# Products of probabilities and values in four column tiles of 32 in place of two of 64

## The chip, the cores and the metric

The kernel runs on one core of one Trainium2 chip. The metric is the device time of one execution in microseconds. The kernel before was timed three times: 3240.45, 3241.63 and 3242.56 us, median 3241.63 us.

## What is computed

The input x has the shape 32 x 56 x 56 x 96 (images, rows, columns, channels), all in float32. Two blocks follow each other; this change touches the first.

```python
x = x + _L0_conv_ref(_gn(x), qkv_w, qkv_b, proj_w, proj_b, rel_table)   # shifted window attention
x = x + _L1_conv_ref(_gn(x))                                            # ratio of box sums
```

The core of the first block, with windows of 7 x 7 (L = 49 tokens), 12 heads and d = 8 channels for each head:

```python
qkv = xw @ qkv_w.T + qkv_b                 # xw: 32 * 64 windows, 49 tokens, 96 channels
q = q * d ** (-0.5)
attn = einsum('bhqd,bhkd->bhqk', q, k) + bias + mask
attn = softmax(attn, axis=-1)
out = einsum('bhqk,bhkd->bhqd', attn, v)   # the product that the change touches
out = out @ proj_w.T + proj_b
```

The second block takes sums over 5 columns and sums over 20 channels of the normalised image and of its square, and adds their ratio.

## The kernel before, in words

The work is cut three ways. An image has 8 units, each a row of 8 windows. A unit has 4 steps, each a pair of windows (w = 0 and w = 1). So there are 32 x 8 x 4 = 1024 steps. A window's 49 tokens lie on partitions 0 to 48, the other window's on 64 to 112.

The program is a software pipeline written out by hand. One loop over slots (L587 on TensorE, and the same loop on each of the other engines) issues in each slot the stages of different steps, in a fixed order; a semaphore per stage holds an engine until its input is there. On TensorE a slot s is, in this order:

- `times_v(s-3)` (L475 to L489): the product of probabilities and values of a step. It writes `pO`, for each of 6 pairs of heads and each of the two windows one matmul: the stationary operand is `P32` (128 rows, the 49 queries of one head for the weights' columns), the moving operand is `V` (18 columns: 8 channels and a one for each of two heads). So 12 matmuls a step, each with its own weights. All operands are float32; the trace shows two weight loads and two matmuls for each matmul of the program, 24 of each a step. The output of window 0 goes to the partitions 0 to 48, that of window 1 to 64 to 112, which are two column tiles of 64 of the array.
- `scores(s+1)` (L446 to L462): 8 bfloat16 matmuls into `pS`, in column tiles of 64 too; first the four of window 0, then the four of window 1. It waits for `biased`, by which VectorE tells that it has read the scores of the step before.
- every fourth slot `values` (L423 to L444): 48 bfloat16 matmuls with 49 columns of weights, which alternate between the two column tiles of 64.
- `turn_scores(s-1)` (L464 to L473): 6 transposes with 128 columns of weights, over the whole width of the array.
- then work that comes once in four slots, all over the whole width: loading and turning x (L394), the box sums (L555, L561, L572, L581), the turned output (L500), the projections (L400 to L402, L510), and small matmuls of the normalisation (L516, L521, L528).

VectorE adds the bias and finds the maximum of the step's scores (L820, L827), GpSimd subtracts it (L1050), ScalarE takes the exponentials into `P32` (L662) and copies from PSUM. Of `pO` nobody reads before the four steps of a unit are done: then VectorE takes the reciprocal of the sums and divides (L850, L857).

Of the kernel before, what the change touches and what calls it, by code (L numbers as in the profile page):

```python
# [15 lines left out]
L = WIN * WIN  # L16
# [10 lines left out]
VC = 2 * (D + 1)  # L27
# [102 lines left out]
def build(nc, x, wT, bias_row, pT, pb_row, flipped, consts, out):  # L130
    ctx = ExitStack()
    with ctx:
        def sb(name, shape, dt=F32):
            return ctx.enter_context(nc.sbuf_tensor(name, shape, dt))

        def psum(name, shape):
            return ctx.enter_context(nc.psum_tensor(name, shape, F32))
# [34 lines left out]
        V = [sb(f"V{i}", [128, UNITS, HP, 2, D + 1]) for i in range(2)]  # L172
        T = [sb(f"T{i}", [128, HEADS, 64]) for i in range(4)]
        MX = [sb(f"MX{i}", [128, HEADS]) for i in range(4)]
        P32 = [sb(f"P32{i}", [128, HEADS, L]) for i in range(3)]
# [27 lines left out]
        pO = psum("pO", [128, 512])  # L203
# [178 lines left out]
        def _(pe):  # L382
# [92 lines left out]
            def times_v(j):  # L475

                U, p = divmod(j, PAIRS)
                pe.wait_ge(p_made, j + 1)
                if p == 0:
                    pe.wait_ge(v_kept, 2 * U + 2)  # L480
                    if U:

                        pe.wait_ge(o_made, U)
                for h in range(HP):
                    col = VC * (HP * p + h)
                    for w in range(2):
                        mm = pe.matmul(pO[64 * w:64 * w + L, col:col + VC], P32[j % 3][:, 2 * h + w, :],  # L487
                                       V[U % 2][:, 2 * p + w, h, :, :], start=True, stop=True)
                mm.then_inc(pv_made, 1)  # L489

            def turn_o(U):
# [95 lines left out]
            for s in range(FIRST_SLOT, END_SLOT + 1):  # L587
                for j in steps(s - 3):
                    times_v(j)
# [515 lines left out]
```

## Time and profile before

| | |
|---|---|
| time of an execution, median of 3 | 3241.63 us |
| span of the profiled execution (first to last instruction) | 3240.4 us |
| TensorE busy | 3157.0 us, 97% |
| VectorE busy | 2883.8 us, 89% |
| ScalarE, GpSimd busy | 70% each |
| granted TensorE clock | 1.00 from 70 to 3160 us |

The profiled execution has no time of its own beside its span; the span stands 1.2 us under the median and inside the three times. PE is TensorE's matmuls, PEld its weight loads. The recorded length of a matmul includes its way through the array (a float32 matmul of 18 moving columns is shown with 200 ns), so lengths of matmuls overlap and their sum tells little. What TensorE spends on a block is read as the difference between the start of the block and the start of the next one in the view in order of time.

### The profile page before, as it was taken

How to read it: one execution, taken by the hardware profiler on the slowest of the kernel's cores; microseconds unless marked ns; L12 is line 12 of the kernel's file. 1: busy time of each engine (PE TensorE's matmuls, PEld its weight loads, DVE VectorE, ACT ScalarE, POOL GpSimd, SP SyncE). 2: the span in 40 equal slices, each digit the busy share in tenths (PEclk: the TensorE clock that was granted, in tenths of full speed). 3: DMA queues.
4: the chain of work that ended last, by engine and by line, in shares of the span. 5: the costliest groups of instructions: out<-in, count | busy, mean ns of one | idle time of the engine just before them, and what ended most of it. 6: DMA issues, size and time to landing. Idle time of an engine off the chain costs nothing.

```text
span 3240.4 us, 146752 instructions
## 1 busy us (share of the span) xinstructions
PE 3157.0 (97%) x60544; PEld 2668.2 (82%) x60544; DVE 2883.8 (89%) x4882; ACT 2282.5 (70%) x4705; POOL 2267.1 (70%) x2522
## 2 busy tenths in 40 slices
PE   4999999999999999999999999999999999999997
PEld 3888888888888888888888888888888888888885
DVE  5999999999999999999999999999999999999983
ACT  2577777777777777777777777777777777777764
POOL 4677777777777777777777777777777777767763
PEclk8999999999999999999999999999999999999995
DMA  3333333333333333333333333333333333333320
GB/s 85 93 84 94 86 89 90 91 87 90 91 87 89 95 85 87 93 89 87 95 86 87 94 88 88 88 92 87 90 93 85 88 95 86 88 97 75 77 65 24
DMA packets 385696, 280.19 MB, mean 86 GB/s; under 512 B 261931, under 2 KB 384908, under 8 KB 385036
## 3 DMA queue, kind: packets, MB, share of 16 engines
q1 hardware_dynamic: 384652, 270.69, 33.9%
q8 instruction: 485, 7.95, 1.1%
q14 instruction: 175, 1.43, 0.1%
q10 hardware_dynamic: 384, 0.11, 0.0%
HBM read 39.35 MB, written 38.54 MB: 24 GB/s over the span
## 4 chain that ended last, share of the span: by engine, by line
PE 92%; ACT 3%; SPq 2%; issue 1%; DVE 1%; DMA 0%; ACTq 0%; POOL 0%; DVEq 0%; POOLq 0%
PE pP L472 22%; PE pO L487 19%; PE pS L460 9%; PE pM L555 6%; PE pM L572 5%; PE pM L510 5%; PE pM L442 5%; PE pM L561 5%; PE pM L394 3%; PE pM L500 3%; PE pM L400 3%; PE pM L401 3%; PE pM L402 3%; PE pM L581 2%; SPq L335 1%
## 5 line engine op out<-in xcount | busy, mean ns | idle before, releaser
L1050 POOL TENSOR_TENSOR T<-T,MX 128x588 f32<-128x588 f32 x1024 | 1212.3, 1185 | 889.8 <-DVE MX L827 886.8
L662 ACT ACTIVATE P<-pP 128x588 f32<-128x588 f32 x1024 | 673.7, 658 | 418.4 <-PE pP L472 411.9
L820 DVE TENSOR_TENSOR T<-pS,table 128x588 f32<-128x588 f32 x1024 | 783.5, 765 | 82.4 <-PE pS L460 53.8
L472 PE MATMUL pP<-K,T 113*128 113x113 f32 x6144 | 818.9, 269 | 0.8 <-ACT P L662 0.8
L827 DVE TENSOR_REDUCE MX<-T 128x12 f32<-128x588 f32 x1024 | 778.3, 760 | 25.9
L487 PEld LDWEIGHTS pO<-V,P 128*49 128x49 f32 x24576 | 646.2, 125 | 162.4 <-ACT P L662 69.2
L487 PE MATMUL pO<-V,P 128*49 128x18 f32 x24576 | 747.1, 200 | 0.4 <-DVE O L857 0.4
L472 PEld LDWEIGHTS pP<-K,T 113*128 113x128 f32 x6144 | 602.6, 141 | 93.3 <-issue 1.0
L460 PE MATMUL pS<-KE,QS 128*64 128x196 bf16 (+1 forms) x8192 | 466.4, 231 | 17.3 <-DMA KE<-KS 16.3
L767 ACT ACTIVATE rd<-pM,tiny 112x384 f32<-112x384 f32 x224 | 130.3, 582 | 362.1 <-PE pM L561 362.0
L460 PEld LDWEIGHTS pS<-KE,QS 128*64 128x64 bf16 x8192 | 309.8, 110 | 18.6 <-DMA KE<-KS 17.0
L652 ACT ACTIVATE V<-pM 49x384 f32<-49x384 f32 x512 | 262.9, 514 | 45.4 <-PE pM L442 39.1
L572 PEld LDWEIGHTS pM<-K,ybox 96*112 96x112 f32 x1792 | 217.9, 183 | 69.5 <-issue 5.9
L1027 POOL TENSOR_TENSOR ybox<-y,Y 96x448 f32<-96x448 f32 x224 | 254.6, 1137 | 17.6
L1015 POOL TENSOR_TENSOR y<-Y 96x472 f32<-96x472 f32 x224 | 217.5, 971 | 41.1 <-ACT Y L739 38.8
L1011 POOL TENSOR_TENSOR XL<-X,XH 96x392 bf16<-96x392 f32 x256 | 238.3, 931 | 0.0
L555 PE MATMUL pM<-K,SQ 96*112 96x96 f32 x1792 | 217.6, 266 | 3.0 <-DVE numt L913 1.9
L572 PE MATMUL pM<-K,ybox 96*112 96x96 f32 x1792 | 216.0, 265 | 0.0
L907 DVE SCALAR_TENSOR_TENSOR numt<-pM,rd 112x384 f32<-112x384 f32 x224 | 125.0, 558 | 100.5 <-PE pM L572 54.1
L510 PE MATMUL pM<-OT,PT 97*96 97x392 f32 x512 | 211.1, 493 | 1.9 <-DVE numt L913 1.9
L1020 POOL TENSOR_TENSOR y<-y 96x448 f32<-96x448 f32 x224 | 208.5, 931 | 0.7
L442 PE MATMUL pM<-WHV,XH 97*49 97x48 bf16 x4096 | 196.1, 184 | 12.6 <-ACT OT L671 12.6
(94 smaller groups left out, 5976.6 us busy)
## 6 DMA issues: line engine op xcount, KB each, us to landing
KE<-KS SPq DMA_DIRECT2D x512, 147.0 KB
KS<-knh SPq DMA_DIRECT2D x768, 49.0 KB
QS<-qnh SPq DMA_DIRECT2D x768, 49.0 KB
out<-tok_out SPq DMA_DIRECT2D x384, 84.0 KB
tok_in<-x SPq DMA_DIRECT2D x224, 84.0 KB
KS<-knl SPq DMA_DIRECT2D x384, 49.0 KB
QS<-qnl SPq DMA_DIRECT2D x384, 49.0 KB
tok_in<-x SPq DMA_DIRECT2D x224, 63.0 KB
```

Of the source, the lines that this page charges most:

```text
L442: mm = pe.matmul(bankA[64 * h:64 * h + L, col:col + C // 2], lhs, wv[:, :, h, :], start=(part == 0), stop=(part == 2))
L460: mm = pe.matmul(pS[64 * w:64 * w + 64, bank, col:col + (h1 - h0) * L], Q[:, gq, at:at + 64], E[:, h0:h1, at:at + L], start=True, stop=True)
L472: mm = pe.transpose(pP[:, c, QN * at:QN * at + QN], T[j % 4][0:QN, 2 * h:2 * h + 2, :], pick)
L487: mm = pe.matmul(pO[64 * w:64 * w + L, col:col + VC], P32[j % 3][:, 2 * h + w, :], V[U % 2][:, 2 * p + w, h, :, :], start=True, stop=True)
L510: pe.matmul(bankB[0:C, 0:TOK], PT[:, :], OT[:, :], start=True, stop=True).then_inc(proj_made, 1)
L555: mm = pe.matmul(bankB[0:ROWS2, C * t:C * t + C], SQ[:, ROWS2 * t:ROWS2 * t + ROWS2], band, start=True, stop=True)
L572: mm = pe.matmul(bankC[0:ROWS2, C * t:C * t + C], ybox2[:, ROWS2 * t:ROWS2 * t + ROWS2], band, start=True, stop=True)
L652: act.activation(V[U % 2][ps, :, :, h, 0:D], bankA[ps, 0:PAIRS * C].rearrange("p (w a d) -> p w a d", w=UNITS, d=D), ACT.Copy).then_inc(v_ ...
L662: act.activation(P32[j % 3][:, :, :].rearrange("p (c a w) q -> p c a (w q)", c=2, w=2), src, ACT.Exp).then_inc(p_made, 1)
L820: dve.tensor_tensor(T[j % 4][:, :, 0:L].rearrange("p (b h) k -> p b h k", b=2), pS[:, :, 0:HALF].rearrange("p b (h k) -> p b h k", k=L), t ...
L827: dve.tensor_reduce(MX[j % 4][:, :], T[j % 4][:, :, 0:L], AX.X, ALU.max).then_inc(maxed, 1)
L1050: pool.tensor_tensor(t, t, MX[j % 4][:, :].unsqueeze(2).broadcast_to([128, HEADS, L]), ALU.subtract).then_inc(shifted, 1)
```

## The change

Each of the 12 matmuls of a step with 49 columns of weights becomes two: one with the queries 0 to 31 (32 columns of weights), one with the queries 32 to 48 (17 columns). The outputs go to the same places in `pO`; window 0 now uses the column tiles of 32 at partitions 0 and 32, window 1 those at 64 and 96. The moving operand is the same, and is streamed for each of them.

```diff
                     for w in range(2):
-                        mm = pe.matmul(pO[64 * w:64 * w + L, col:col + VC], P32[j % 3][:, 2 * h + w, :],
-                                       V[U % 2][:, 2 * p + w, h, :, :], start=True, stop=True)
+                        for q0, q1 in ((0, 32), (32, L)):
+                            mm = pe.matmul(pO[64 * w + q0:64 * w + q1, col:col + VC], P32[j % 3][:, 2 * h + w, q0:q1],
+                                           V[U % 2][:, 2 * p + w, h, :, :], start=True, stop=True)
                 mm.then_inc(pv_made, 1)
```

No semaphore, buffer or stage moves, and the other engines' programs are the same. Only TensorE's list of instructions differs. In the order of the program, TensorE before, around one product (the first figure of a form is the number of weight columns, the second that of moving columns):

```order
L572 MATMUL pM<-K,ybox 112x96 x4
L500 MATMUL pM<-K,O 96x113 x4
L487 MATMUL pO<-V,P 49x18 x12
L460 MATMUL pS<-KE,QS 64x196
L460 MATMUL pS<-KE,QS 64x98 x2
```

This is the order that a step has: full-width work, one group of 12 with equal forms, and at once the scores.

In the changed kernel, where such a product begins (lines after L487 are one further on: L501 is L500, L573 is L572):

```order
L573 MATMUL pM<-K,ybox 112x96 x4
L501 MATMUL pM<-K,O 96x113 x4
L488 MATMUL pO<-V,P 32x18
L488 MATMUL pO<-V,P 17x18
L488 MATMUL pO<-V,P 32x18
L488 MATMUL pO<-V,P 17x18
```

The work ahead is unchanged; the product now opens with a 32-column matmul of window 0 and its 17-column rest, then the same for window 1. And where it ends and the scores begin:

```order
L488 MATMUL pO<-V,P 32x18
L488 MATMUL pO<-V,P 17x18
L460 MATMUL pS<-KE,QS 64x196
L460 MATMUL pS<-KE,QS 64x98 x2
L460 MATMUL pS<-KE,QS 64x196 x2
```

So the 12 matmuls of a step are 24, of 32 and 17 columns in turn, and what stands before and behind them is the same; the scores behind them stay in column tiles of 64.

## Rows read from the trace of the kernel before

**Rows 1.** The page, parts 1 and 2: busy time, and the granted TensorE clock by slices.

```profile
PE 3157.0 (97%) x60544; PEld 2668.2 (82%) x60544; DVE 2883.8 (89%) x4882; ACT 2282.5 (70%) x4705; POOL 2267.1 (70%) x2522
...
PEclk8999999999999999999999999999999999999995
```

**Rows 2.** The page, part 4: the chain of waits that ended last, by engine and line.

```profile
PE 92%; ACT 3%; SPq 2%; issue 1%; DVE 1%; DMA 0%; ACTq 0%; POOL 0%; DVEq 0%; POOLq 0%
PE pP L472 22%; PE pO L487 19%; PE pS L460 9%; PE pM L555 6%; PE pM L572 5%; PE pM L510 5%; PE pM L442 5%; PE pM L561 5%; PE pM L394 3%; PE pM L500 3%; PE pM L400 3%; PE pM L401 3%; PE pM L402 3%; PE pM L581 2%; SPq L335 1%
```

**Rows 3.** Stretches (start-up, middle, tail): busy us (x instructions) by engine, PE clock, DMA.

```profile
core 0: us, PE busy (x) PEld busy (x) DVE busy (x) ACT busy (x) POOL busy (x), PEclk, DMA share, GB/s
0.00:70.00 70.00, 25.72 (x175) 17.15 (x176) 33.47 (x49) 18.05 (x41) 27.74 (x44) 0.88 0.33 81
70.00:3160.00 3090.00, 3073.65 (x60107) 2607.30 (x60107) 2825.64 (x4788) 2229.34 (x4597) 2211.65 (x2449) 1.00 0.36 88
3160.00:3240.40 80.40, 57.62 (x272) 43.74 (x268) 24.71 (x47) 35.08 (x69) 27.67 (x30) 0.55 0.09 24
```

**Rows 4.** The waits: engine and line waiting, releaser, us in total, times, longest.

```profile
POOL T L1050 <- DVE MX L827: 886.8, 737, 35.5
...
DVE T L820 <- PE pS L460: 53.8, 221, 10.2
...
PE pS L460 <- DMA KE<-KS: 16.3, 5, 13.8
```

**Rows 5.** The page, part 5: groups of instructions (columns as the page's heading says).

```profile
L487 PEld LDWEIGHTS pO<-V,P 128*49 128x49 f32 x24576 | 646.2, 125 | 162.4 <-ACT P L662 69.2
L487 PE MATMUL pO<-V,P 128*49 128x18 f32 x24576 | 747.1, 200 | 0.4 <-DVE O L857 0.4
```

**Rows 6.** TensorE in order of time: start us, us, engine, line, instructions merged.

```profile
1602.36 0.55 PE L500 MATMUL pM<-K,O 113*96 113x113 f32 x4
1602.84 0.73 PE L487 MATMUL pO<-V,P 128*49 128x18 f32 x24
1603.41 0.46 PE L460 MATMUL pS<-KE,QS 128*64 128x196 bf16 x8
1603.67 0.21 PE L442 MATMUL pM<-WHV,XH 97*49 97x48 bf16 x2
...
1604.28 0.18 PE L442 MATMUL pM<-WHV,XL 97*49 97x48 bf16 x1
1604.28 0.18 PE L442 MATMUL pM<-WLV,XH 97*49 97x48 bf16 x1
1604.31 0.18 PE L442 MATMUL pM<-WHV,XL 97*49 97x48 bf16 x1
1604.42 0.80 PE L472 MATMUL pP<-K,T 113*128 113x113 f32 x6
1605.06 0.82 PE L510 MATMUL pM<-OT,PT 97*96 97x392 f32 x2
...
1606.14 0.73 PE L487 MATMUL pO<-V,P 128*49 128x18 f32 x24
1606.71 0.46 PE L460 MATMUL pS<-KE,QS 128*64 128x196 bf16 x8
1607.10 0.80 PE L472 MATMUL pP<-K,T 113*128 113x113 f32 x6
1607.73 0.33 PE L400 MATMUL pM<-XH,WH 97*96 97x392 bf16 x1
...
1610.42 0.55 PE L394 MATMUL pM<-K,tok_in 112*96 112x112 f32 x4
1610.80 0.94 PE L555 MATMUL pM<-K,SQ 96*112 96x96 f32 x8
1611.67 0.50 PE L487 MATMUL pO<-V,P 128*49 128x18 f32 x14
```

**Rows 7.** Groups by form: weight loads of 112, 49 (bf16) and 96 columns.

```profile
L555 PEld LDWEIGHTS pM<-K,SQ 96*112 96x112 f32 x1792 | 199.9, 183 | 5.2 <-issue 4.4 <-ACT g L695 0.8
...
L442 PEld LDWEIGHTS pM<-WLV,XH 97*49 97x49 bf16 x4096 | 175.2, 103 | 0.0
...
L510 PEld LDWEIGHTS pM<-OT,PT 97*96 97x96 f32 x512 | 67.0, 164 | 2.5 <-issue 2.1
```

**Rows 8.** Groups by form: the scores' matmuls, wide and narrow.

```profile
L460 PE MATMUL pS<-KE,QS 128*64 128x196 bf16 x4096 | 466.4, 256 | 17.3 <-DMA KE<-KS 16.3 <-DVE T L820 0.9
L460 PE MATMUL pS<-KE,QS 128*64 128x98 bf16 x4096 | 285.0, 206 | 0.0
```

## The prediction

> **What bounds the kernel now.** I first read busy shares, then the chain of waits, then the waits themselves, then TensorE in order of time. TensorE is busy 97% of the span at the full granted clock of 2.4 GHz, VectorE 89% [rows 1]. The chain that ended last runs 92% of the span through TensorE, and the line that changes, L487, holds 19% of it, the second largest share [rows 2]. Between 70 and 3160 us TensorE is idle only 3090.0 - 3073.7 = 16 us; VectorE is idle 3090.0 - 2825.6 = 264 us there [rows 3]. The long waits are those of others for TensorE or for each other; TensorE's own longest is 16.3 us for the first transfers, and VectorE waits 53.8 us in all for the scores [rows 4]. So TensorE is the bound throughout: what a step saves or costs on its engine comes through nearly one to one, until VectorE's 264 us are used up.
>
> **What a product costs now.** The busy sums don't tell it: 24576 matmuls of 200 ns would be more than the whole span, they lie over each other [rows 5]. The starts do. A product begins at 1602.84 and the scores behind it at 1603.41: 0.57 us for 24 matmuls; 1606.14 to 1606.71 again [rows 6]. Two things about this 0.57 us decide the case.
>
> First, the two column tiles run side by side. The scores are written as four matmuls of window 0 and then four of window 1, 4 x 196 + 4 x 98 = 1176 moving columns [rows 8], which at 2.4 GHz in a line are 0.49 us; they take 0.26 us (1603.41 to 1603.67) [rows 6]. So TensorE takes the second tile's work ahead while the first is busy. In the product each tile then has 12 load-and-matmul pairs in 0.57 us, 47.5 ns each.
>
> Second, it is the weight load that sets these 47.5 ns. The 18 moving columns are fewer than the 49 columns of weights. A float32 load grows with its columns: 125 ns recorded for 49 [rows 5], 164 for 96, 183 for 112 [rows 7]. In spacing rather than in recorded length: the eight loads of 112 columns at L555 take 1610.80 to 1611.67, 0.87 us, of which 0.095 us is the change of tiling worked out below, so 97 ns each against 47.5 ns for 49 columns: (97 - 47.5) / 63 = 0.79 to 0.81 ns for a column [rows 6].
>
> **The change, part by part.** (a) Narrower loads. A tile with 32 columns saves 17 x 0.81 = 13.8 ns in each of its 12 slots of time: 33.7 ns in place of 47.5. The tiles with 17 columns need 47.5 - 32 x 0.81 = 21.6 ns and are done before, if all four tiles run side by side. Saving 12 x 13.8 = 166 ns a step.
>
> (b) Twice as many instructions, 48 load-and-matmul pairs a step in place of 24. Within 12 x 33.7 = 404 ns that is one pair each 8.4 ns. No row shows such a pace. The nearest is L442, 48 pairs whose starts lie between 1603.67 and 1604.31, 0.64 us for 47 spacings, 13.6 ns each, and there two tiles' matmuls start at the same hundredth (both at 1604.28) [rows 6]; a tile's own spacing is 27 ns there, close to what 49 bfloat16 columns need, so 13.6 ns is a pace that was reached and not a limit that was met. Bounds for the product: 404 ns if the pace is no limit (a little less if narrow tiles had a lower floor than I assume, 12 x 27 = 324 ns), and 48 x 13.6 = 653 ns if 13.6 ns were the least. I take the 404, because the equal starts speak against a shared minimum and because the engine was seen to run different tiles independently.
>
> (c) One more change of tiling. The product is bracketed today by full-width work ahead and by the scores behind, which use the same column tiles of 64. Before a change of tiling a block gets longer: four transposes of 112 columns (L394) take 1610.42 to 1610.80 when full-width work follows, four of 113 (L500) take 1602.36 to 1602.84 when the product follows: 0.38 and 0.48 us; starts are shown to 10 ns, so the loss is 0.09 to 0.11, and I take 0.095. And the six transposes at L472 right behind such a change take 1604.42 to 1605.06, 0.64 us, where 6 x 0.096 = 0.58 would do: up to 0.055 us more for a first load that nothing hides [rows 6]. From the product to the scores there is no such loss now. With tiles of 32 in front of tiles of 64 there would be one in each step. Bounds: 0 (as between equal tilings) and 0.095 + 0.055 = 0.15 us. I take 0.095 + 0.020, since the scores' load is half as wide as L472's, and about 10 ns for four tiles in place of two that have to be started one after another: 125 ns.
>
> Here a rule of the Trainium skill bears. What the rows show is the loss between tiles of 64 and the full width. TensorEngine Tiling, Key Properties, states it in general: a change of the tiling mode, not just of the tile, drains the engine. The trace agrees where it can; whether 32 after 64 counts as such a change no row shows. By the rule the term is the 125 ns above, without it about 10 ns.
>
> Nothing else moves: no wait is added, `pO` is read by VectorE only once in four steps, and the same semaphore is raised by the last matmul. The granted clock should stay at 2.4 GHz, for TensorE works without a pause before and after.
>
> **Sum.** A step: -166 + 125 = -41 ns. 1024 steps: -42 us. VectorE's 264 us of slack cover it, so all of it should come through. From the profiled execution's 3240.4 us: 3198 us; the median of the runs stands 1.2 us above that, so 3200 us.
>
> **The rivals.** *No loss between tiles of 64 and 32.* Step: -166 + 10 = -156 ns, 160 us in all. For it: both are column tilings over all 128 rows, and a tile of 64 covers just two of 32. Against it: the loss at the full width. VectorE's work would then be 2826 of some 2930 us and would begin to hold single steps, so I take nine tenths: 3241.6 - 144 = about 3097 us.
>
> *A common pace of loads and matmuls.* The place is the product alone; the price is 48 x pace against 570 ns before, plus the 125 ns. It decides from 48 x pace = 570 - 125, or 9.3 ns a pair: above it the kernel gets slower. At 13.6 ns: 653 + 125 - 570 = +208 ns a step, +213 us, 3455 us; at 11 ns +85 us, 3327 us. The same comes out if only two tiles can take weights at a time: 12 x (33.7 + 21.6) = 664 ns. For it: nowhere in the trace do more than two column tiles work at a time. Against it: the equal starts.
>
> Beside this rival: TensorE: Matmul & The Clock Gate, in its table of the isolated gap, puts a floor of about 25 ns on the start-to-start time of small matmuls. If it held over all tiles the product would take 48 x 25 = 1200 ns, a step 1200 + 125 - 570 = 755 ns more and the kernel 4015 us, an estimate from that page; the trace disagrees, since L442 starts one each 13.6 ns [rows 6], and only a floor within one tile is left of it, which 33.7 ns respects.
>
> *Gain and loss cancel.* With a pace near 9 ns, or the extra change at its full 0.15 us and a tile of 32 at 37 ns, the sum is zero: 3241 us. That the change doesn't do what it says is excluded by the order: the forms 32x18 and 17x18 alternate.
>
> **How the numbers follow.** The forecast of some -10 to -75 us (around 3200 us, its own range 3165 to 3230) gets 0.46. No loss between the tilings 0.15. Common pace above 9.4 ns 0.27, spread from 3250 to 3460 us. Cancelling 0.12. About 0.2%, 6.5 us, is what a measurement of this kernel can tell from no change. Faster: 0.46 + 0.15, less 0.01 for its edge, 0.60; same 0.12; slower 0.28. The range leaves out the upper half of the pace case and a little below the second: 3090 to 3345 us.
>
> **What would show it.** Right: product to scores about 0.52 us (0.40 for the loads, the rest the loss) in place of 0.57, four tiles' matmuls in bundles 34 ns apart, the loads of 32 columns recorded with about 111 ns and those of 17 with 99, scores and transposes behind them unchanged. The loss between tilings shown wrong: 0.41 us from product to scores. The pace shown: 0.65 us or more, with single matmuls evenly spaced. What would make the prediction wrong elsewhere: TensorE idle before L460 or L472 in the middle stretch, which would be VectorE's or ScalarE's doing.

## The result and the profile after

The changed kernel takes 3227.30 us (median of 4 runs, 3223.82 to 3230.10), the kernel before in the same job 3241.36 us (3240.45 to 3242.56). The ratio is 0.9955, with a 95% interval of 0.9943 to 0.9968: faster by 14 us or 0.45%, a third of the 42 us that were forecast. One thing is seen before any trace is opened: the runs of before lie within 2.1 us of each other, those after within 6.3 us.

The page after (parts 1, 3, 4 and 5; of queue q8, which brings the instructions, the columns are packets, MB, share of 16 engines):

```profile
PE 3123.7 (97%) x85120; PEld 2599.5 (81%) x85120; DVE 2870.6 (89%) x4882; ACT 2282.8 (71%) x4705; POOL 2267.8 (70%) x2522
...
q8 instruction: 677, 11.09, 1.5%
...
PE 93%; ACT 3%; issue 2%; DVE 1%; ACTq 0%; SPq 0%; POOL 0%; DMA 0%; POOLq 0%; DVEq 0%
PE pP L472 23%; PE pO L488 16%; PE pS L460 12%; PE pM L556 6%; PE pM L573 5%; PE pM L511 5%; PE pM L442 5%; PE pM L562 5%; PE pM L394 3%; PE pM L501 3%; PE pM L400 3%; PE pM L401 3%; PE pM L402 3%; PE pM L582 2%; PE pM L529 1%
...
L488 PE MATMUL pO<-V,P 128*32 128x18 f32 (+1 forms) x49152 | 610.5, 184 | 13.5 <-issue 12.5
```

and q8 on the page before:

```profile
q8 instruction: 485, 7.95, 1.1%
```

TensorE is still the bound, 93% of the chain [rows 2]. The changed line went from 19% to 16% of it, the scores behind it from 9% to 12%. A cause of idle time has come up at L488 that had none there before: 12.5 us of "issue", time in which TensorE waited for nothing that the profile shows. And 192 more packets of instructions were fetched. TensorE has 49152 more loads and matmuls than before, and q8 has 3.14 MB more: 64 bytes an instruction, 256 instructions a packet.

The middle stretch, for [rows 3]:

```profile
70.00:3145.00 3075.00, 3040.91 (x84627) 2538.61 (x84626) 2812.30 (x4786) 2229.45 (x4596) 2212.37 (x2449) 1.00 0.37 90
```

TensorE is idle 34 us there against 16, while VectorE's share is what it was.

TensorE in order of time, two undisturbed products, for [rows 6]:

```profile
1604.98 0.33 PE L402 MATMUL pM<-XH,WL 97*96 97x392 bf16 x1
1605.24 0.59 PE L488 MATMUL pO<-V,P 128*32 128x18 f32 x48
1605.76 0.46 PE L460 MATMUL pS<-KE,QS 128*64 128x196 bf16 x8
1606.15 0.80 PE L472 MATMUL pP<-K,T 113*128 113x113 f32 x6
1606.79 0.55 PE L394 MATMUL pM<-K,tok_in 112*96 112x112 f32 x4
1607.17 0.94 PE L556 MATMUL pM<-K,SQ 96*112 96x96 f32 x8
1608.04 0.59 PE L488 MATMUL pO<-V,P 128*32 128x18 f32 x48
1608.56 0.46 PE L460 MATMUL pS<-KE,QS 128*64 128x196 bf16 x8
1608.95 0.80 PE L472 MATMUL pP<-K,T 113*128 113x113 f32 x6
```

From the product to the scores it is 0.52 us both times (1605.24 to 1605.76, 1608.04 to 1608.56) where it was 0.57. From the scores to the transposes it is 0.39 us as before, or finely 8 ns more. The weight loads by form (mean ns behind the busy us), for [rows 5]:

```profile
L488 PEld LDWEIGHTS pO<-V,P 128*32 128x32 f32 x24576 | 505.0, 110 | 170.9 <-ACT P L663 69.2 <-issue 59.5
L488 PEld LDWEIGHTS pO<-V,P 128*17 128x17 f32 x24576 | 488.6, 95 | 8.1 <-issue 7.8
```

110 ns for 32 columns and 95 for 17, against 125 for 49.

Over the whole trace, by the differences of the blocks' starts: the median of 1020 products went from 571 to 520 ns; the scores before transposes from 385 to 393 (767 times), before values from 265 to 286 (255 times), the values from 748 to 734. In sum -52.0 + 6.1 + 5.4 - 3.6 = -44 us. The spans differ by 14.6 us. So 29.5 us were gained and lost again, and not in the usual step. The next view shows where; it is a product that took 1.60 us in place of 0.52:

```profile
1354.23 0.55 PE L501 MATMUL pM<-K,O 113*96 113x113 f32 x4
1354.71 0.44 PE L488 MATMUL pO<-V,P 128*32 128x18 f32 x32
1356.07 0.31 PE L488 MATMUL pO<-V,P 128*32 128x18 f32 x16 [0.92 <-issue]
1356.31 0.46 PE L460 MATMUL pS<-KE,QS 128*64 128x196 bf16 x8
```

In the middle of it, between two matmuls that wait for no semaphore, TensorE stood for 0.92 us. Such waits come up in the view of waits (us in total, times, longest). The trace before has not one row of this kind ("issue") for the matmuls:

```profile
PE pO L488 <- issue: 12.5, 24, 1.0
...
PE pS L460 <- issue: 4.1, 9, 1.0
...
PE pM L442 <- issue: 1.5, 3, 0.7
...
PE pP L472 <- issue: 0.4, 1, 0.4
```

A recorded matmul runs on for 0.18 us after its start, so that each idle time is shown shorter than the stall was, and short ones not at all. Measured from start to start, there are 58 gaps between 0.17 and 1.16 us beyond the usual spacing (the median of the same pair of forms), 28.8 us in all: the missing sum. All 58 stand at the same place: when the loads, matmuls and semaphore instructions of TensorE's program are counted, the instruction behind the gap is the 197th to 204th of a group of 256, nearly all the 197th to 199th. In the trace before, the gaps of this size are spread over all places, and are the waits at the start of an image. 256 instructions are one packet of q8, and the program of TensorE has as many such groups as q8 has packets: 677 after, 485 before.

### The profile page after: what moved, and what is told of

Read it like the earlier page. It is cut to its first block, busy times and chain, and to the rows that moved or that the text cites. A ratio compares the mean times of both kernels' runs of the same rounds, so it can differ in the third digit from the quotient of the medians.

```text
span 3225.8 us, 195904 instructions
## 1 busy us (share of the span) xinstructions
PE 3123.7 (97%) x85120; PEld 2599.5 (81%) x85120; DVE 2870.6 (89%) x4882; ACT 2282.8 (71%) x4705; POOL 2267.8 (70%) x2522
## 4 chain that ended last, share of the span: by engine, by line
PE 93%; ACT 3%; issue 2%; DVE 1%; ACTq 0%; SPq 0%; POOL 0%; DMA 0%; POOLq 0%; DVEq 0%
PE pP L472 23%; PE pO L488 16%; PE pS L460 12%; PE pM L556 6%; PE pM L573 5%; PE pM L511 5%; PE pM L442 5%; PE pM L562 5%; PE pM L394 3%; PE pM L501 3%; PE pM L400 3%; PE pM L401 3%; PE pM L402 3%; PE pM L582 2%; PE pM L529 1%
## 5 line engine op out<-in xcount | busy, mean ns | idle before, releaser
L472 PE MATMUL pP<-K,T 113*128 113x113 f32 x6144 | 820.0, 270 | 2.1 <-ACT P L663 1.0
L472 PEld LDWEIGHTS pP<-K,T 113*128 113x128 f32 x6144 | 603.1, 141 | 95.4 <-issue 2.7
L488 PEld LDWEIGHTS pO<-V,P 128*17 128x17 f32 (+1 forms) x49152 | 505.6, 103 | 179.0 <-ACT P L663 69.2
L488 PE MATMUL pO<-V,P 128*32 128x18 f32 (+1 forms) x49152 | 610.5, 184 | 13.5 <-issue 12.5
L460 PE MATMUL pS<-KE,QS 128*64 128x196 bf16 (+1 forms) x8192 | 478.0, 234 | 19.9 <-DMA KE<-KS 14.3
L460 PEld LDWEIGHTS pS<-KE,QS 128*64 128x64 bf16 x8192 | 292.9, 109 | 53.2 <-DMA KE<-KS 14.5
L573 PEld LDWEIGHTS pM<-K,ybox 96*112 96x112 f32 x1792 | 217.9, 183 | 69.5 <-issue 6.2
L573 PE MATMUL pM<-K,ybox 96*112 96x96 f32 x1792 | 216.0, 265 | 0.0
```

The lines of the kernel that those rows point to most:

```text
L460: mm = pe.matmul(pS[64 * w:64 * w + 64, bank, col:col + (h1 - h0) * L], Q[:, gq, at:at + 64], E[:, h0:h1, at:at + L], start=True, stop=True)
L472: mm = pe.transpose(pP[:, c, QN * at:QN * at + QN], T[j % 4][0:QN, 2 * h:2 * h + 2, :], pick)
L488: mm = pe.matmul(pO[64 * w + q0:64 * w + q1, col:col + VC], P32[j % 3][:, 2 * h + w, q0:q1], V[U % 2][:, 2 * p + w, h, :, :], start=True, ...
L573: mm = pe.matmul(bankC[0:ROWS2, C * t:C * t + C], ybox2[:, ROWS2 * t:ROWS2 * t + ROWS2], band, start=True, stop=True)
```

## The experiments

Theory A, formed from this: TensorE runs out of instructions. A group of 256 must last until the next one is fetched and usable. In the 56 stalled groups that could be measured, the packet was fetched 1.7 us (median) after the group before was begun, took 1.0 us, and TensorE went on 1.4 us after its end, together some 4.2 us. Before, the quickest of all groups lasted 4.4 us; after, the quickest lasts 3.3 us. From the 20th group on, TensorE begins no group in any trace of this case sooner than 1.1 us after the end of the packet that was fetched during the group ahead; in the trace before, the least is 2.0 us, so that it never came near this bound. A quick group need not stall: most of those under 4.2 us did not, and their fetch began earlier (0.4 us after the group's beginning, median, against 1.6 to 1.7 in the stalled ones). The theory's rival B: the time is lost by the four tiles themselves, by the changes of tiling, or by other engines that fall behind. All ratios are to the kernel before, timed in the same job, and each edit is one of the changed kernel unless it is said otherwise. The stalls are told from one profiled execution of each kernel.

**24 products of 32 columns** (the count of instructions as before, tiles of 32).

```diff
-                        for q0, q1 in ((0, 32), (32, L)):
+                        for q0, q1 in ((0, 32),):
```

> Leaves out the queries 32 to 48 of each product, so a step has 24 load-and-matmul pairs of 32 columns, as many instructions as before, in tiles of 32. Theory A (instruction supply): the changed kernel lost about 27 us in some 56 stretches in which TensorE had used up its instructions; with the count of before these go. The product's block stays at 0.50 to 0.52 us, no idle time of TensorE put down to issue at L488, time 3185 to 3202 us. Theory B (the lost time comes from the four tiles, the changes of tiling or other engines falling behind, not from the number of instructions): the long blocks stay in part, time 3210 us or more.

Measured: 3174.17 us, ratio 0.9793 (0.9779 to 0.9806). In order of time:

```profile
1602.91 0.56 PE L488 MATMUL pO<-V,P 128*32 128x18 f32 x24
1603.41 0.46 PE L460 MATMUL pS<-KE,QS 128*64 128x196 bf16 x8
1603.80 0.80 PE L472 MATMUL pP<-K,T 113*128 113x113 f32 x6
```

The block takes 0.50 us (median of all 490 ns), and there is no idle time put down to issue for any matmul. The time is under the range that A gave, since the block was 30 ns shorter than the one with four tiles; B's 3210 us is excluded. This kernel has half the instructions in the product, but also two tiles in place of four; which of the two takes the stalls away the next experiments tell.

**24 products of 33 columns** (the same, in tiles of 64).

```diff
-                        for q0, q1 in ((0, 32), (32, L)):
+                        for q0, q1 in ((0, 33),):
```

> Leaves out the queries 33 to 48 of each product: 24 pairs of 33 columns, which need column tiles of 64 as before, and so no further change of tiling before the scores. If the change of tiling costs about 0.1 us a step and the load of 33 columns is as good as that of 32: the block takes 0.41 to 0.42 us against 0.50 to 0.52 with 32 columns alone, time 3080 to 3105 us. If a change between tiles of 64 and 32 costs nothing and the loads themselves are slower than forecast: 0.50 us here too, and 3185 to 3200 us.

Measured: 3109.78 us, ratio 0.9602 (0.9587 to 0.9617).

```profile
1602.08 0.57 PE L488 MATMUL pO<-V,P 128*33 128x18 f32 x24
1602.49 0.45 PE L460 MATMUL pS<-KE,QS 128*64 128x196 bf16 x8
1602.87 0.80 PE L472 MATMUL pP<-K,T 113*128 113x113 f32 x6
```

0.41 us from product to scores, 0.08 less than with 32 columns, although each load is one column wider. So there is a price for going from tiles of 32 to tiles of 64: 490 - 411 + 10 for the wider column in 12 loads + 8 in the scores, 0.10 us in all. And 16 columns fewer in 12 loads gave 571 - 411 = 160 ns, 0.83 ns a column. The step's gain, 164 us over 1024 steps, did not all come through: the total fell by 131 us. The scores before the values became longer, from 265 to 333 ns; I put this down to the values, which now wait for ScalarE's copies. The trace bears it out: the first weight load of the values starts 113 to 115 ns behind the end of the copy at L672 in nearly all units, where it is 151 ns (median) in the trace of before. No run tests it.

**32 columns and 1** (instructions and tiles as after, hardly any work in two of the tiles).

```diff
-                        for q0, q1 in ((0, 32), (32, L)):
+                        for q0, q1 in ((0, 32), (32, 33)):
```

> Leaves out the queries 33 to 48: each product is issued as 32 columns and 1 column, with as many instructions and the same tiles as in the changed kernel, but next to no work in the second and fourth tile. Theory A: the same stalls, 20 to 30 us of idle time put down to issue, time 3217 to 3230 us. Theory B, in the form that the loads of 17 columns crowd out those of 32: the stalls go, 3185 to 3200 us.

Measured: 3234.47 us (3228.89 to 3243.66), ratio 0.9979 (0.9969 to 0.9990).

```profile
PE pO L488 <- issue: 13.5, 24, 1.2
...
PE pS L460 <- issue: 3.9, 10, 0.6
...
PE pM L442 <- issue: 3.1, 6, 0.8
```

The stalls are all there, 71 gaps with 34 us at the same place of the groups of 256, and the block is 520 ns, as with 17 columns. Between this kernel's span and that of the one with 32 columns alone stand 62.5 us: 31 us for a block that is 30 ns longer, and 32 us more of stalls (34 against 2 at most), for 24576 more loads and as many more matmuls with a single column. The width of the added matmuls doesn't matter. That it is their number, and not the four tiles, is shown by the place in the groups of 256 and by the runs that follow. It came out 4 us above the range that A gave, the number of stalls being greater than I had assumed.

**The second step of each unit undivided.** The slot of this product also has the 48 matmuls of the values.

```diff
-                        for q0, q1 in ((0, 32), (32, L)):
+                        for q0, q1 in (((0, L),) if p == 1 else ((0, 32), (32, L))):
```

> Complete. The product of the second step of each unit, which stands in the slot with the 48 matmuls of the values and so in the densest stretch of instructions, stays undivided (49 columns, two tiles of 64); the other three are divided. Theory A: three quarters of the steady gain of 43 us a kernel (32 us) and hardly a stall: 3207 to 3213 us, faster than both. Theory B: three quarters of the gain measured, about 3231 us.

Measured: 3215.77 us, ratio 0.9924 (0.9911 to 0.9936).

```profile
PE pO L488 <- issue: 0.6, 2, 0.4
...
PE pP L472 <- issue: 0.6, 1, 0.6
```

Faster than both kernels, with a quarter fewer divided products. 15 gaps with 5.7 us are left; for 9 of them, 3.3 us, TensorE goes on within 1.7 us of the end of a packet, as in the stalls above. It is 3 us above A's range and 15 under B's value.

**The first step undivided instead**, the same number of instructions in the program.

```diff
-                        for q0, q1 in ((0, 32), (32, L)):
+                        for q0, q1 in (((0, L),) if p == 0 else ((0, 32), (32, L))):
```

> Complete. As p1_undivided, but it is the first step's product in each unit that stays undivided; as many instructions and as much steady gain, only the slot differs: this one has no values. If the stalls come from the number of instructions as such: 3216 us, like p1_undivided. If they come from dense stretches (the slot with the values and the one before it): more stalls than p1_undivided, 8 to 18 us of them, 3218 to 3226 us.

Measured: 3235.96 us (3231.76 to 3240.55), ratio 0.9982 (0.9973 to 0.9991).

```profile
PE pO L488 <- issue: 5.8, 16, 0.8
...
PE pM L442 <- issue: 3.4, 6, 1.0
...
PE pS L460 <- issue: 2.7, 6, 0.8
```

44 gaps with 21 us. Both kernels have the same instructions in number and kind, and differ by 19 us (by the ratios; they were timed in different jobs) by where the dense ones stand. It is not the sum of instructions that matters, but how quickly 256 in a row are used up. The median lies above my range, and even the profiled execution, 33 us of steady gain less 21 of stalls, comes to a span of 3228 by this sum against the measured 3231.9; so I can't account for the last few microseconds.

**Two divided products together** in every second slot, which halves the changes from tiles of 32 to 64.

```diff
                 for j in steps(s - 3):
-                    times_v(j)
+                    if j % 2:
+                        times_v(j - 1)
+                        times_v(j)
```

> Complete. The divided products of two steps are issued one behind the other in every second slot, so the change of tiling before the scores comes 512 times and not 1024. Without a limit on instructions this should save about 0.1 us on every second step, 50 us: 3175 us. Theory A (instruction supply): the two products, the scores and, in every second such slot, the values are 304 instructions in about 2 us, where a block of 256 instructions was not seen to be followed by the next in less than about 3.3 us; so a stall of 1 to 2 us in most units of steps, TensorE idle for issue 200 us or more, and slower than the changed kernel: 3300 us or more.

Measured: 3501.54 us, ratio 1.0803 (1.0787 to 1.0819): 8% slower, by the same instructions in another order.

```profile
1608.53 1.15 PE L488 MATMUL pO<-V,P 128*32 128x18 f32 x96
1609.60 0.46 PE L460 MATMUL pS<-KE,QS 128*64 128x196 bf16 x8
1609.89 0.20 PE L442 MATMUL pM<-WHV,XH 97*49 97x48 bf16 x2
...
1611.32 0.21 PE L442 MATMUL pM<-WHV,XH 97*49 97x48 bf16 x2 [0.70 <-issue]
1611.34 0.21 PE L442 MATMUL pM<-WLV,XH 97*49 97x48 bf16 x2
1611.37 0.21 PE L442 MATMUL pM<-WHV,XL 97*49 97x48 bf16 x2
1611.50 0.80 PE L472 MATMUL pP<-K,T 113*128 113x113 f32 x6
```

Two products take 1.07 us together here (median 0.99), the scores behind them 0.29, and then the values, which are 0.73 us elsewhere, last from 1609.89 to 1611.50, with TensorE idle for 0.70 us in the midst. Among the waits:

```profile
PE pO L488 <- issue: 82.3, 96, 2.1
PE pM L442 <- issue: 77.1, 90, 2.4
...
PE pS L460 <- issue: 24.0, 32, 1.7
```

Up to 3100 us of the span that is some 230 gaps with 220 to 230 us, and up to its end 266 gaps with 261 us. This is where the theories lay farthest apart, 3175 against over 3300 us.

Not all of the 260 us above the kernel before are stalls. The middle stretch:

```profile
70.00:3420.00 3350.00, 3101.68 (x84740) 2571.07 (x84740) 2813.31 (x4791) 2257.77 (x4600) 2222.55 (x2454) 0.99 0.34 82
```

TensorE is idle for 248 us here, and the granted clock is 0.99 where it was 1.00 in the traces before and after: it fell to its lower level (1.2 GHz) in 18 stretches of 3.4 to 10.2 us, 92 us in all. At half speed this costs at most 46 us, an estimate. Against it stand the blocks, which are some 68 us shorter in sum than in the kernel before. In the other kernels with stalls it stood there for 0 to 6.8 us in all. So the time of this kernel isn't a measure of the stalls alone.

**Two undivided products together.** The same edit on the kernel before.

> Complete. The same pairing with undivided products (49 columns, two tiles of 64), where no change of tiling is to be saved: 208 instructions in 2.1 us in every second such slot. Without a limit on instructions: 3241 us, unchanged. Theory A: some stalls, between 3245 and 3300 us, clearly fewer than with divided products.

Measured: 3258.36 us, ratio 1.0052 (1.0037 to 1.0067). In the range, but not for A's reason: only 10 gaps with 3.5 us. In 6 of them TensorE goes on 1.3 to 1.6 us after the end of a packet, as in the stalls above, and this with tiles of 64 alone: four tiles aren't needed for such a stall. What is new are waits for VectorE:

```profile
PE pS L460 <- DVE T L822: 20.7, 40, 0.9
...
PE pM L400 <- DVE WL L895: 10.0, 30, 1.2
```

Of the 40 waits of the scores 38 stand behind the block at L394, in a slot without a product: there the scores come sooner than VectorE has read the last ones. So the pairing costs about 17 us by itself. With it the divided pairs add up: 261 us of stalls, up to 46 of clock and 17 of pairing, less 68, are at most 256 us, and the spans of the two kernels differ by 256 us.

**Less data moved**, in the changed kernel and in the one before.

```diff
-                    sp.dma_start(KE[b][rows, i::HQ, :], KS[rows, :, :]).then_inc(staged, 16)
+                    sp.dma_start(KE[b][rows, i::HQ, 0:L], KS[rows, :, 0:L]).then_inc(staged, 16)
```

> The changed kernel with the last staging transfer (KE from KS) cut to its first 49 of 784 columns, which leaves out most of the copied keys, some 70 of 271 MB. If transfers of data delay the fetches of instructions and so make the stalls: fewer stalls, 3205 to 3215 us. If the fetches take their time whatever else is moved: 3222 to 3230 us, with some 25 us of stalls.

> The kernel before with the same staging transfer cut, as the control: TensorE waits for this transfer only at the start, so 3235 to 3242 us by either theory.

Measured: 3218.08 us, ratio 0.9927 (0.9912 to 0.9942), and for the kernel before 3238.92 us, ratio 0.9993 (0.9984 to 1.0003). Between both expectations: with 27% less data moved in queue q1 the stalls fell from 58 gaps with 28.8 us to 45 with 22.5 us, 6 us, and the total by 9 us where the control fell by 3. A packet of instructions took the same 1.13 us (mean) in both. So other transfers have some part in it, in what way is not shown, and most of the stall is there with a quarter less of them.

**Wide tiles first**, in the changed kernel and with the second step undivided.

```diff
-                    for w in range(2):
-                        for q0, q1 in ((0, 32), (32, L)):
+                    for q0, q1 in ((0, 32), (32, L)):
+                        for w in range(2):
```

> Complete. The changed kernel with the four matmuls of a pair of heads in another order: 32 columns of window 0, 32 of window 1, then the two rests of 17. The block with four tiles was seen to be 0.52 us where two tiles of 32 alone take 0.49. If part of these 30 ns is the third tile being started late and running out of sight behind the rests: block 0.505 to 0.515 us, 5 to 15 us faster than the changed kernel, 3212 to 3222 us. If the order does not matter, because each tile's work is taken ahead anyway: 0.52 us and 3227 us.

> Complete. Both: the second step's product undivided and the wide tiles first in the others. 3205 to 3212 us if the order helps, 3216 us if not.

Measured: 3232.25 us (3229.47 to 3235.80), ratio 0.9968 (0.9956 to 0.9980), and 3215.60 us (3212.46 to 3219.36), ratio 0.9914 (0.9897 to 0.9930). The block fell by 3 ns only, from 520 to 517, which is 3 us in all, and the stalls were more (71 gaps with 34 us against 58 with 28.8). So the order within a product gives nothing that can be told from no change. The 30 ns between four tiles and two lie inside the product: from its first matmul to its last it is 410 ns with four tiles and 376 with two of 32 columns, and from the last to the scores 110 and 114. The matmuls of 32 columns start at the same pace in both at first, and the time is lost in the last third, when those of 17 have stopped running ahead. Why stays open.

## Why the prediction was wrong

- What bounds the kernel: right. TensorE before and after, and what a step gained came through as far as TensorE had instructions.
- (a) Narrower loads, -166 ns a step at 0.81 ns a column: right. With 33 columns, where nothing else changes, it was 0.83 ns a column; within the divided product a tile's 32-column matmuls start 31.7 ns apart against the 33.7 forecast, and some 33 in its last part. Its own rows give 0.79 rather than 0.81. And the recorded lengths that it names, 125, 164 and 183 ns, don't show a growth with the columns alone, for another float32 load of 96 columns is recorded with 129 ns (the line below, from the trace of before); the spacings carried the term:

```profile
L394 PEld LDWEIGHTS pM<-K,tok_in 112*96 112x96 f32 x1024 | 108.8, 129 | 25.9 <-DMA PT<-pb_row 16.9 <-issue 7.6 <-ACT g L695 0.8
```

- (b) The pace: the four tiles do run side by side, and the block was not at 653 but about as forecast; the rival of a common pace fell, and with it the bound of two tiles at a time. Four tiles in place of two cost 30 ns, not the 10 that stood in (c).
- (c) The change of tiling: 125 ns forecast, 10 of them for the start of four tiles. Measured 100 for the change, and the 30 above, 130 together. The row for 64 against full width carried over to 32 against 64, with 0.10 us by the two kernels with 32 and 33 columns. The Trainium skill states a drain of the engine for such a change of mode in general (TensorEngine Tiling, Key Properties); these two kernels agree with it.
- The sum of the usual step: -41 ns forecast, -43 ns measured; over all steps -42 us and -44 us. Up to here the mechanism and its size were right.
- The step that failed is "Nothing else moves". I counted the doubled instructions only as work for the array, and bounded (b) by paces inside of TensorE. Each of them has also to be brought there, 64 bytes each, and the trace of before had what was needed to see it: q8's 485 packets of 16 KB, and the spans of time in which 256 instructions were used up, 4.4 us at the least. With 96 instructions for the product and 96 for the values side by side it was to be asked what happens when these spans become 3.3 us. That term is worth +29 us, and it is two thirds of the forecast gain. The runs showed it four ways: gone with half the instructions, still there (34 us) with instructions that do hardly any work, moved by 19 us with the place of the dense slot, and nine times as large when two products stood together.
- The rivals: none of those I named was the one that came. The range was wide for the pace and for the change of tiling, which both came out near their terms. That 3227.3 us still lies in the range of the main case, 3165 to 3230, is luck. The sign named for an error elsewhere, TensorE idle before L460 or L472, did show, with 4.1 and 0.4 us, but the cause put to it, VectorE or ScalarE, was not the one.
- A small slip without effect: TensorE's longest wait before was not the 16.3 us for `KE` but 16.9 us for `PT`, at the start too.

## What to carry to other kernels

When an edit multiplies small instructions, don't only price them on the engine: take the densest stretch of the new program, see how long 256 instructions last there, and compare it with the shortest such stretch that the trace of before has got through without idle time put down to "issue". Where it falls below, a stall becomes possible; keep the denser form out of the stretches that are full already; here that took one condition on the step and made 3215.8 of 3227.3 us (and 3241.4 before). A median over repeated blocks tells whether the mechanism works, and the mean less the median tells what it has cost elsewhere.

## What the runs showed of the hardware that I had not expected

- Instructions reach TensorE in packets of 16 KB or 256 instructions, and a group that is used up in less than about 4.2 us can be followed by a stall of 0.2 to 1.4 us (up to 2.6 us with two products together). The start of the fetch varies by a microsecond and more. The runs spread over 6.3 us after against 2.1 before; that the fetches make this spread is not shown.
- In tiles of 32 columns TensorE runs four streams side by side: the 17-column matmuls of a tile start 25 ns apart and run ahead of the 32-column ones, which keep to 31.7 ns. Even with a single column the 25 ns stay. This lasts for two thirds of the product; then the narrow ones pause for some 60 ns, and all go on at 33 ns. The 48 pairs of a product start within 410 ns, 8.7 ns each.
- A change between column tiles of 32 and 64 costs TensorE 0.10 us (490 ns with 32 columns against 411 with 33, the wider column and the scores' 8 ns added), as much as the 0.09 to 0.11 us read for 64 against the full width.
- The granted clock can fall in short stretches inside a dense program: with TensorE idle for 248 of 3350 us in pauses of up to 2.6 us, it stood at its lower level for 92 us.
